# Four small loads on another queue, new written orders on four engines, and more idle products, in a two-block attention kernel on one core

## The reference

```
# block 1, on x of shape (4, 192, 32, 32), N = 1024 pixels
xn  = layer_norm(x[:, :48])                       # over 48 channels
q, k, v = split(bn(w_qkv @ xn), [16, 16, 48])
attn = softmax(q.T @ k * 16 ** -0.5)              # 1024 x 1024
out  = v @ attn.T
y    = bn(w_proj @ relu(concat(out, x[:, 48:])))
# block 2, heads of 24 channels: attention over channels
q, k, v = qkv_w @ x;  q, k = l2norm(q), l2norm(k)
at   = softmax(q @ k.T * temperature) @ v         # 24 x 24 per head
conv_x = depthwise3x3(conv1x1(v))
t    = conv1x1(at)                                # 192 -> 32 channels
ci1  = conv1x1(mean(t));  ci2 = conv1x1(depthwise7x7_dilated3(depthwise3x3(t)))
channel_map = conv1x1(t * ci1 * ci2)              # its mean gates conv_x
sp   = conv1x1(gelu(x1) * x2), x1, x2 = split(depthwise3x3(conv1x1(conv_x)))
                                                  # its sigmoid gates at
```

## Time and profile before

| | |
|---|---|
| median of 3 runs | 376.67 us (372.95, 376.67, 381.56) |
| profiled execution, its own time | 377.97 us |
| its span, first to last instruction | 376.0 us |
| mean granted clock of TensorE | 0.916 of full |
| busy: PE / PEld / DVE / ACT / POOL | 342.3 / 169.2 / 258.0 / 185.1 / 28.4 us |
| DMA | 12.37 MB |

### The profile page before, as it was taken

The page is one execution under the profiler, slowest core; times in us unless marked ns, Lnnn a source line. Parts: engine busy times, 40 slices in busy tenths (PEclk is TensorE's granted clock), DMA queues, the critical chain, the costliest instruction groups (busy, mean ns, idle before and its releaser), DMA issues.

```text
span 376.0 us, 5306 instructions
## 1 busy us (share of the span) xinstructions
PE 342.3 (91%) x2114; PEld 169.2 (45%) x2114; DVE 258.0 (69%) x471; ACT 185.1 (49%) x324; POOL 28.4 (8%) x35
## 2 busy tenths in 40 slices
PE   6869897999999999989999999999999878797995
PEld 4626453243336643553353646453245355252431
DVE  4544756834178737758998487789775999586363
ACT  3413525764642348745852587438515665347220
POOL 3210010000002110002000120001000004000000
PEclk9975567999998579999999999999999999699999
DMA  8810000000000000130000213000002130013005
GB/s 251 276 42 0 0 0 2 1 0 2 0 0 3 0 0 2 32 64 2 1 2 0 84 32 65 2 2 0 0 11 75 31 67 2 0 31 65 2 0 167
DMA packets 6069, 12.37 MB, mean 33 GB/s; under 512 B 2078, under 2 KB 2718, under 8 KB 5918
## 3 DMA queue, kind: packets, MB, share of 16 engines
q1 hardware_dynamic: 5388, 11.75, 11.3%
q10 hardware_dynamic: 658, 0.29, 0.4%
HBM read 5.32 MB, written 3.15 MB: 23 GB/s over the span
## 4 chain that ended last, share of the span: by engine, by line
PE 67%; ACT 10%; issue 8%; DMA 6%; DVE 5%; POOL 1%; POOLq 1%; SPq 1%; ACTq 1%; DVEq 0%
ACT pT L2061 4%; PE psR L823 3%; PE psO L648 3%; PE psA L638 3%; DMA up<-up 2%; PE psS L648 2%; DMA bn2h<-params_dram 2%; PE psO L572 2%; PE psA L619 2%; PE psA L823 2%; PE psB L691 2%; ACT up L2161 2%; DMA wt<-params_dram 1%; PE psA L671 1%; PE psA L558 1%
## 5 line engine op out<-in xcount | busy, mean ns | idle before, releaser
L1570 DVE SCALAR_TENSOR_TENSOR dd<-spp,wt,dd 112x1024 f32<-112x1024 f32 x32 | 41.0, 1281 | 0.9 <-ACT dd L2182 0.2
L1559 DVE SCALAR_TENSOR_TENSOR cx<-cpA,dw2w,cx 128x1024 f32<-128x1024 f32 x32 | 40.9, 1277 | 0.0
L2061 ACT ACTIVATE pT<-psA 128x1024 f32<-128x1024 f32 x24 | 24.5, 1023 | 15.0 <-PE psA L638 15.0
L1416 DVE TENSOR_REDUCE nmp<-psA 128x2 f32<-128x1024 f32 x20 | 24.5, 1223 | 6.7 <-PE psA L619 6.6
L648 PE MATMUL psO<-pT,vt 128*64 128x512 f32 x96 | 25.8, 616 | 0.2
L1559 DVE SCALAR_TENSOR_TENSOR cx<-cpB,dw2w,cx 128x512 f32<-128x512 f32 x32 | 23.8, 744 | 1.4 <-ACT cx L2101 1.4
L823 PE MATMUL psR<-up,wb 128*32 128x256 f32 (+1 forms) x336 | 20.5, 382 | 1.4 <-DMA up<-up 1.4
L2444 POOL TENSOR_TENSOR gr<-gvar,mhalf 128x2 f32<-128x2 f32 x8 | 7.0, 874 | 144.4 <-DVE gvar L1358 144.4
L2444 POOL TENSOR_TENSOR rn<-nrm,mhalf 96x4 f32<-96x4 f32 x4 | 9.2, 2312 | 102.7 <-DVE nrm L1478 102.7
L823 PEld LDWEIGHTS psR<-up,wb 128*32 128x32 f32 (+1 forms) x336 | 9.7, 109 | 10.9 <-issue 3.6
L2074 ACT ACTIVATE xm<-x 128x1024 f32<-128x1024 f32 (+1 forms) x8 | 6.7, 838 | 15.8 <-PE psO L678 11.8
(11 more groups left out here) (444 smaller groups left out, 744.4 us busy)
## 6 DMA issues: line engine op xcount, KB each, us to landing
up<-up SPq DMA_DIRECT2D x12, 200.0 KB, 3.1
x<-x_dram SPq DMA_DIRECT2D x4, 512.0 KB, 7.1
out_dram<-x SPq DMA_DIRECT2D x8, 256.0 KB, 2.1
wt<-params_dram SPq DMA_DIRECT2D x1, 1151.5 KB, 7.7
tp<-tp SPq DMA_DIRECT2D x8, 136.0 KB, 2.4
x<-x_dram SPq DMA_DIRECT2D x8, 128.0 KB, 7.1
out_dram<-x SPq DMA_DIRECT2D x8, 128.0 KB, 2.3
wt<-params_dram ACTq DMA_DIRECT2D x1, 213.5 KB, 5.2
```

What stands on the lines that cost most here:

```text
L1416: v.tensor_reduce(s.nmp[:, n, i:NKT:4], score_ps[b][t % 2][:].rearrange("p (r k) -> p r k", r=2), AX_X, ALU.max, negate=True).then_inc(nm_ ...
L1559: v.scalar_tensor_tensor(acc, img, dw2w[:, blk, tap:tap + 1], acc, ALU.mult, ALU.add).then_inc(cv_s.of(c), 1)
L1570: v.scalar_tensor_tensor(acc, t.spp[:, dy:dy + HH, dx:dx + WW], par("w_spdw")[:, tap:tap + 1], acc, ALU.mult, ALU.add).then_inc(dv_s.of(c), 1)
L2061: a(s.pT[t % 2][:], s.scoreT_ps[:], ACT.Exp, scale=QK ** -0.5).then_inc(ex_s.of(b), 1)
```

## The change

`load_small` is issued by SP, between the loads of image 1 and the second part of the parameters, and no longer by ACT, behind `normed1(0)`. The lists of PE, DVE and ACT are written in another order in many places; POOL's list is the same. Idle products are 19 instead of 16 as `keep_warm`, and nine of a new kind, `keep_hot`, write the upper half of psR. ACT's first zeroing of a back tile waits for the first part of the parameters by itself. No other step is added or taken out.

```diff
+            def load_small():
+                off, cols = AT["wdw2"][1], 18 + VECS
+                sp.dma_start(rawa[0:CH, :], params[0:CH, off:off + cols]).then_inc(s_vec, 16)
...
             load_x(0)
             load_x(1)
+            load_small()
             sp.dma_start(wt[:, N1:N2], params[:, N1:N2]).then_inc(s_w2, 16)
...
+            def keep_hot():
+
+                mm(psR[:, HB:N][:, 0:QB], ident, wt[:, 0:QB], start=True, stop=True)
...
             setup_ln()
             keep_warm()
+            keep_warm()
             group_means(0, 0)
-            keep_warm()
-            keep_warm()
-            keep_warm()
+            setup_qkv()
...
-                if i and k == 0:
-                    act.wait_ge(*x2_s(B - 1, 2))
+                if k == 0:
+                    act.wait_ge(*((s_w1, 16), x2_s(B - 1, 2))[i])
...
             normed1(0)
-            load_small()
+            zero_back(0, 0)
             squares(0)
```

More of the change, by code:

```diff
@@ L933, in _ @@
             keep_warm()
-            setup_qkv()
             pixel_var(0)
@@ L1074, in _ @@
             pv(2, 4)
+            scores_t(2, 6)
+            ci2b(0, 3)
+            pv(2, 5)
+            scores_t(2, 7)
             ci2b(0, 4)
             ci2b(0, 5)
-            scores_t(2, 6)
-            pv(2, 5)
             ci2b(0, 6)
+            pv(2, 6)
+            pv(2, 7)
             sp_out_a(0)
-            scores_t(2, 7)
-            pv(2, 6)
+            denominators(2)
             map_mean(0)
-            pv(2, 7)
+            denominator_rows(2)
             sp_out_b(0)
-            denominators(2)
             attended_a(0)
-            denominator_rows(2)
-            transpose_attn(1)
             attended_b(0)
@@ L1092, in _ @@
             proj2_a(0)
+            transpose_attn(1)
+            group_means(1, 2)
             proj2_b(0)
[L1094 removed]
+            group_means(0, 3)
             attn_weights(1)
[L1096 removed]
             sp_in(1)
@@ L1181, in _ @@
             ci2b(2, 4)
+            norms(3)
+            sp_out_a(2)
             ci2b(2, 5)
+            ci2b(2, 6)
             k_norm_rows(3)
-            ci2b(2, 6)
             sp_in(3)
-            sp_out_a(2)
             transpose_attn(3)
@@ L1605, in _ @@
             channel_stats(0, 2)
+            setup_ln()
             moments(0)
+            setup_qkv()
             group_stats(0, 0)
@@ L1609, in _ @@
             normed1_half()
-            setup_qkv()
             setup_weights()
+            channel_stats(1, 0)
             pixel_var(0)
-            channel_stats(1, 0)
             channel_stats(1, 1)
+            channel_stats(1, 2)
+            moments(1)
+            layer_norm(0)
             setup_bias()
             setup2_a()
-            layer_norm(0)
-            channel_stats(1, 2)
-            moments(1)
-            channel_stats(2, 0)
+            group_stats(0, 1)
             q_low(0)
             k_low(0)
-            channel_stats(2, 1)
-            group_stats(0, 1)
+            channel_stats(2, 0)
             v_copy(0)
+            group_shift(0, 1)
             row_max(0, 0)
             row_max(0, 1)
-            group_shift(0, 1)
             row_max(0, 2)
@@ L1647, in _ @@
             row_max(1, 2)
-            moments(2)
             row_max(1, 3)
@@ L1667, in _ @@
             normed(0)
+            moments(2)
+            channel_stats(3, 0)
             inverse_denominators(1)
@@ L1697, in _ @@
             conv2(0, 15)
+            scaled_scores(0)
             pixel_var(2)
-            scaled_scores(0)
+            channel_stats(3, 1)
             softmax_divide(0)
+            layer_norm(2)
             copy_wma(0)
-            layer_norm(2)
+            channel_stats(3, 2)
+            moments(3)
             copy_wmc(0)
@@ L1714, in _ @@
             row_max(2, 4)
-            sp_conv(0, 0)
-            sp_conv(0, 1)
+            conv2(1, 0)
             row_max(2, 5)
+            conv2(1, 1)
             gram_copy(1, 0)
@@ L1723, in _ @@
             times_w(1)
+            sp_conv(0, 0)
+            sp_conv(0, 1)
             clamp_norms(1)
             sp_conv(0, 2)
+            sp_conv(0, 3)
+            conv2(1, 2)
             inverse_norms(1)
-            sp_conv(0, 3)
-            conv2(1, 0)
             sp_conv(0, 4)
+            conv2(1, 3)
+            conv2(1, 4)
             sp_conv(0, 5)
@@ L1732, in _ @@
             sp_conv(0, 7)
-            scale_t(0)
-            conv2(1, 1)
-            conv2(1, 2)
-            gelu_product(0, 0)
-            gelu_product(0, 1)
-            conv2(1, 3)
-            conv2(1, 4)
-            channel_product(0)
             conv2(1, 5)
@@ L1765, in _ @@
             result(0, 0)
+            group_stats(1, 2)
             result(0, 1)
-            group_stats(1, 2)
             result(0, 2)
@@ L1868, in _ @@
             conv2(3, 9)
+            conv2(3, 10)
+            gelu_product(2, 0)
+            gelu_product(2, 1)
             clamp_norms(3)
-            sp_conv(2, 7)
-            conv2(3, 10)
             conv2(3, 11)
+            conv2(3, 12)
             inverse_norms(3)
-            conv2(3, 12)
             conv2(3, 13)
@@ L2334, in _ @@
             pad_sp(1, 1)
+            normed2(2)
             sp_first(1)
             pad_t(1)
+            squares(3)
             copy_t(1)
-            squares(3)
             center_copy(3)
@@ L2373, in _ @@
             exps(3, 6)
+            exps(3, 7)
             copy_k_norms(2)
-            exps(3, 7)
             attn_out(3)
```

284 lines of the change are left out of this document (144 added, 140 removed).

## The result

The changed kernel took 360.62 us (median of 4 runs, 356.95 to 366.09) beside 377.16 us for the kernel before in the same measurement (4 runs, 372.95 to 381.56). The ratio is 0.9565, 95% interval 0.9425 to 0.9704; 361.5 us had been forecast. Two later measurements, on two chips, gave 0.9591 (0.9485 to 0.9698) and 0.9643 (0.9596 to 0.9690).

A forecast was written before the change was run, and what follows sets the result against it. The start was taken as bound by an unneeded small load, then by PE at half clock, later by PE's work. Steps of 3.9, 1.8, 2.4, 5.3, 1.3, 1.7 and 0 sum to 16.4: 377.97 - 16.4 = 361.5 us, range 355 to 371.

The forecast's parts named there:

- Step 1: Start up to q: small loads issued earlier and a new order around xn make q 3.9 us earlier.
- rival three: Clock falls in the first 20 us, where that work then takes 8.8 us more: 381.6 us, chance 0.05.
- rival five: Small loads arrive late anyway, with only `q_low(0)` behind them: 1 us lost, 362.5 us, chance 0.03.
- Steps 2 and 3: q and k at full clock, 1.8 us; first row scores no longer behind three idle products, 2.4 us.
- Step 4: Image 0's maxima, first row scores to `scores_t(0, 0)`: 14.4 us at full clock, limited by DVE; 5.3 us gained.
- rival one: Clock falls in image 0's score rows all the same, costing 7.0 us: 368.5 us, chance 0.25.
- Step 5: From `scores_t(0, 0)` up to image 1's hand-over, `max_rows(1)`: reordered work on PE gains 1.3 us.
- Step 6: Image 0's front, up to the transposed head softmax, at full clock: 1.7 us gained, upper bound 5.7 us.
- Rival two: Image 0's front stays at half clock, nine idle products making it 7.5 us longer: 370.7 us, chance 0.13.
- Step 7: All other moves, including those near the end: 0, between 2 us better and 3 us worse.
- rival four: New orders cost waits in images 1 to 3, some 3 to 4 us: 365 us, chance 0.14.

The follow-up runs named there:

- e_load_back: The changed kernel with the four small loads back on ACT, behind `normed1(0)`: 366.85 us, ratio 0.9752.
- c_after: The changed kernel run again, unchanged, with a second profile: 357.05 us, ratio 0.9591.
- e_setup2_back: The changed kernel with `setup2` moved back behind `score_rows(0, 7)`: 363.09 us, ratio 0.9761.
- e_mid: The changed kernel with four more idle products (`keep_mid`) in image 0's score rows: 361.22 us, ratio 0.9546.
- e_no_hot: The changed kernel without its nine `keep_hot` idle products: 362.07 us, ratio 0.9707.
- e_order_only: The changed kernel with the small loads back on ACT and without the nine `keep_hot`, leaving the new orders: 367.32 us, ratio 0.9779.
- c_after2: The changed kernel unchanged, as a control on the third chip: 359.16 us, ratio 0.9643.

## Why the prediction came out right, and where it did not

The time, 360.62 against 361.5 us, and the reason, more of the span at full clock, were right: some 61 us were at 1.2 GHz before, and 33, 10 and 14 us in the three profiles of the changed kernel, so the length of half clock didn't just move, which the prediction named as its sign of being wrong. The terms were not all right, and they made up for each other.

**Step 1** (3.9 us) holds in the execution that didn't fall at the start: q at 19.65 us, 4.2 earlier. In the execution profiled first only 1.5 us came, because the clock had fallen by 15.5 us. That is rival three's mechanism, priced there at 8.8 us: from the two profiles of the same kernel it cost 22.33 - 19.65 = 2.7 us up to q and 47.50 - 43.15 = 4.35 us up to `scores_t(0, 0)`, since it fell during `pixel_var(0)` and not at 7.4 us; some of it may have gone into PE's idle time. The price for loads that stay late, 1 us (rival five), was mis-sized: 2.34 us of wait and 2.4 us later row scores in e_load_back, and 4 to 7 us more in the whole by the ratios (0.9752 against 0.9565 to 0.9643), 6.6 us by the mean spans, most of it by the clock. The slip: `q_low(0)` was put at about 22 us; with q at 20 us it is due before that, at 21.56 us in c_after.

**Steps 2 and 3** (4.2 us together) measured 4.0 us at full clock and 2.4 at half.

**Step 4** (5.3 us) failed in its size, as the clock that it took to be full was not, and rival one was there at less than its price. In every profile of the changed kernel itself the clock fell in the score rows (35.8, 31.5 and 30.5 us), and 2.1 us came of 5.3. Rival one asked for 7.0 us more than the forecast; it was 3.2, as the piece lasted 10 to 11 us and not 29.8. The limit of 14.4 us at full clock was sound: 14.1 us in e_setup2_back, 15.4 in e_mid. It overlooked that `setup2` now stands ahead of the eighth row scores; 1.3 us between those two are that and the four idle products, which weren't separated.

**Step 5** (1.3 us) measured 3.3 us in both profiles. The half clock of 60.8 to 67.6 us is gone, and image 1's eight maxima follow one another without those waits: in c_after they start from 52.06 to 60.40 us, 1.19 us apart. The sum had taken 7.8 us for the last five with `max_rows`, a row in which DVE still waited for PE; from the first row scores (51.52 us) to `max_rows(1)` (62.28) it was 10.8 us where the sum had 12.1.

**Step 6** (1.7 us, bound 5.7) measured 4.8 us. The nine products took 0.5 us each as forecast. That they would hide held only in part: two of them stand ahead of `gram_w(0)`, where from `group_means(1, 1)` to it are 2.87 us with them (106.16 to 109.03 us) and 2.25 us in e_no_hot (103.83 to 106.08 us), and at equal clock the nine cost 2.0 us. Rival two isn't seen in any profile with nine of them. The 1.7 was a sure part only. How it divides: the front without them but with 6.5 us at half clock took 14.46 us, with them 13.19, and before, with 17.2 us at half clock, 18.00. So the 4.8 us aren't all the nine products' work: in e_no_hot's profile 3.5 us of them are there without any.

**Step 7** (0, from -2 to +3) measured +2.1 and -2.2 us in two executions of one kernel, with some 10 us of half clock near 310 us and with none, where the kernel before had some 7 us. A loss of the size of rival four, a wait in images 1 to 3, is not in the second.

The sum by sections for the profiled pair is 376.0 - 364.0 = 12.0 us, for the second execution 20.7 us; 16.4 lay between. Of the signs that the prediction named, `scores_t(0, 0)` near 40 us was missed in all three profiles (47.50, 43.15 and 42.46 us), and q near 20 us in the first. The single number also started from the profiled 377.97 us, 1.3 us over the median that it was to forecast. That it was so near is partly luck: the range 355 to 371 us was the honest part (its lower end takes all three of its reasons together, though it says "or": 361.5 - 2.9 - 2 - 1.3 = 355.3 us), and executions of the changed kernel filled it from 355.46 to 367.38 us.

**The new queue.** The small loads were issued at 4.2 to 6.1 us in place of 12.4 to 14.4 us, and DVE's wait went with it. Whether the earlier issue did it or the queue isn't shown, as no run moved the one without the other; so none tests the rule of the Trainium skill (DMA: Bandwidth & Descriptors, section "Issuing engines are not separate DMA queues"), by which the issuing engine alone saves no more than issue time, and none speaks against it.

## What to carry to other kernels

When two versions differ in their granted clock, put span against clock for single executions of each first: here the slope, 2.77 us for each .01, told that 13.8 of 16.3 us went with the clock, which no comparison of two profiles could. A price for idle products has two sides, what they cost at equal clock (2.0 us for nine, 2.1 us for the four more of e_mid) and the clock that comes with them (4.2 us and 0.7 us); measure both, for more of them needn't pay. And before you say that a wait is harmless where it has been moved to, look when the next step on that engine is due once everything ahead is faster.

## What the runs showed of the hardware

The clock fell without a long wait of PE, and stayed low where PE was hardly idle. In c_after it fell just after 31.5 us, after a stretch in which PE was busy 8.81 of 11.50 us with no wait for another engine above 1.45 us (in the kernel before it fell within the 3.4 us in which PE did nothing), and the 11 us that follow, PE busy 10.97 of them, were at 1.2 GHz. The fall came during `pixel_var(1)`, products of two columns each, and in the first profile during `pixel_var(0)`; but in e_order_only it came at some 12.8 us, while PE waited 1.10 us for the normalised image, behind idle products. Nor does the stretch ahead decide it alone: from 7.40 to 15.50 us PE was busy 6.44 us in the first profile, whose clock fell, and 6.74 us in c_after, whose clock did not. The Trainium skill (TensorE: Matmul & The Clock Gate, section "Why this matters for your kernels") advises against idle gaps of TensorE between bursts of products. These falls came with short waits only, in c_after 1.45 us at most, so by this case's rows it doesn't cover them all. With nine idle products in the front none of nine profiles fell there, without them all four did, and the one with four of them did for a shorter time. What the chip counts is not shown.

Executions of one kernel on one chip differed by 10 us (c_after2: 357.14 to 367.38, clocks of .986 to .952; the kernel before on the first chip: 369.31 to 380.57, clocks of .949 to .909), on the line of the others.
